# Moving a mixture's router scores from normalised rows at its start to raw rows at the end of the stage before it

## The reference

```python
def _layernorm(x, axis=-1, eps=1e-05):
    m = jnp.mean(x, axis=axis, keepdims=True)
    v = jnp.var(x, axis=axis, keepdims=True)
    return (x - m) / jnp.sqrt(v + eps)
...
x = x + 0.5 * _L0_ffn_ref(_layernorm(x), ...)     # three linear maps, tanh
x = x + _L0_attn_ref(_layernorm(x), ...)          # gated linear attention
x = x + 0.5 * _L0_ffn_ref(_layernorm(x), ...)
x = x + 0.5 * _L1_ffn_ref(_layernorm(x), ...)     # mixture, 1 of 8 experts
x = x + _L1_attn_ref(_layernorm(x), ...)
x = x + 0.5 * _L1_ffn_ref(_layernorm(x), ...)
x = x + 0.5 * _L2_ffn_ref(_layernorm(x), ...)     # mixture, 2 of 8 experts
x = x + _L2_attn_ref(_layernorm(x), ...)
x = x + 0.5 * _L2_ffn_ref(_layernorm(x), ...)
... # L3: dense experts, attention, dense experts
def _L1_ffn_ref(x, router_w, router_b, w1, b1, w2, b2, game_emb):
    logits = jnp.einsum('bsh,he->bse', x, router_w) + router_b
    expert_idx = jnp.argmax(logits, axis=-1)
    ... # each token's row through its expert: gelu((x + 0.1*game) @ w1 + b1) @ w2 + b2
def _L2_ffn_ref(x, router_w, w1, w2):
    probs = jax.nn.softmax(xf @ router_w.T, axis=-1)
    topv, topi = jax.lax.top_k(probs, 2)
    ... # the two experts' outputs, weighted
```

## Time and profile before

| | us |
|---|---|
| three runs, median | 1935.78 |
| three runs, lowest and highest | 1935.43 and 1937.0 |
| the profiled execution | 1927.49 |
| its span, first to last instruction | 1925.7 |
| around the span | 1.8 |

### The profile page before, as it was taken

How to read it: one execution, slowest core, us unless ns; L and a number is a source line. 1 busy time by engine, 2 the same in 40 slices (tenths; PEclk the granted TensorE clock), 3 DMA queues, 4 the chain that set the end, 5 groups by cost and what they waited for, 6 DMA issues and landing times. The chain is left out here.

```text
span 1925.7 us, 27869 instructions
## 1 busy us (share of the span) xinstructions
PE 1505.0 (78%) x9104; PEld 825.5 (43%) x9104; DVE 1106.2 (57%) x2420; ACT 918.3 (48%) x2114; POOL 358.5 (19%) x514
## 2 busy tenths in 40 slices
PE   4795748999999493882899999973883948999667
PEld 3344643555555482881222222223773532222345
DVE  6576432333433526215988888957214758878466
ACT  3553334444444151223688888761222327777422
POOL 0230630000000170771311010000671001100000
PEclk7796878999999595896899999995896978999878
DMA  2003444020200454546122020003452042220000
GB/s 70 5 1 94 140 127 99 1 66 5 61 1 1 136 145 124 155 135 172 41 42 68 10 77 1 1 1 97 135 150 72 1 129 77 78 77 1 1 0 22
DMA packets 96335, 126.08 MB, mean 65 GB/s; under 512 B 14773, under 2 KB 65973, under 8 KB 95693
## 3 DMA queue, kind: packets, MB, share of 16 engines
q1 hardware_dynamic: 86540, 105.26, 19.3%
q0 software_dynamic: 7936, 16.27, 3.1%
q10 hardware_dynamic: 1728, 2.88, 0.7%
HBM read 87.57 MB, written 36.80 MB: 65 GB/s over the span
## 5 line engine op out<-in xcount | busy, mean ns | idle before, releaser
L1944 DVE TENSOR_REDUCE MAXI<-psum 128x2 f32<-128x1024 f32 x384 | 457.2, 1219 | 91.0 <-PE psum L1752 88.1
L1861 ACT ACTIVATE EX<-psum 128x512 f32<-128x512 f32 x768 | 412.8, 605 | 104.6 <-PE psum L1773 104.5
L1773 PE MATMUL psum<-QM,KM 64*128 64x512 bf16 x768 | 227.2, 384 | 28.9 <-ACT EX L1861 21.7
L2209 PE MATMUL psum<-EX,N 128*128 128x512 f32 x512 | 237.6, 607 | 0.0
L2267 ACT ACTIVATE EX<-psum 128x512 f32<-128x512 f32 x256 | 149.4, 599 | 173.2 <-PE psum L2201 173.2
L1752 PE MATMUL psum<-KM,QS 64*128 64x512 bf16 x768 | 184.7, 401 | 37.1 <-DVE MAXI L1944 15.5
L1783 PE MATMUL psum<-EX,VST 128*32 128x512 f32 x1536 | 203.1, 604 | 1.0 <-ACT OT L1875 1.0
L1048 POOL DMA_INDIRECT m_XG<-rows,m_ROWS x124 | 121.8, 983 | 389.3 <-DVE m_ROWS L1263 352.7
L1080 PE MATMUL psum<-m_XT,m_W 128*128 128x128 f32 x992 | 144.0, 291 | 23.7 <-DVE m_XT L1294 19.0
L1301 DVE TENSOR_SCALAR m_Y<-psum 128x128 f32<-128x128 f32 x124 | 36.1, 291 | 215.7 <-DMA y<-m_Y,m_ROWS 136.0
L285 PE MATMUL psum<-ident,N 128*128 128x128 f32 x192 | 46.1, 406 | 138.1 <-DVE N L249 137.8
(11 more groups left out here) (303 smaller groups left out, 2127.6 us busy)
## 6 DMA issues: line engine op xcount, KB each, us to landing
m_W<-in_w_dram SPq DMA_DIRECT2D x124, 256.0 KB, 2.9
parts<-PART SPq DMA_DIRECT2D x36, 256.0 KB, 2.3
m_DOWN<-in_w_dram SPq DMA_DIRECT2D x32, 256.0 KB, 4.7
parts<-PART SPq DMA_DIRECT2D x12, 384.0 KB, 2.5
parts<-PART SPq DMA_DIRECT2D x36, 128.0 KB, 2.1
rows<-N SPq DMA_DIRECT2D x16, 256.0 KB, 4.7
N<-y SPq DMA_DIRECT2D x16, 256.0 KB, 4.1
parts<-FIX SPq DMA_DIRECT2D x16, 256.0 KB, 3.0
```

What stands on the lines that cost most here:

```text
L1773: pe.matmul(bank_of(("score", n, i)), KM[r, buf, g, m, kt * P:(kt + 1) * P], QM[r, n % 2, MAPS[at] // slots, :], start=True, stop=True).th ...
L1861: act.activation(EX[:, n % 2, kt, MAPS[j], :], bank_of(("score", n, i)), ACT.Exp, scale=SM_SCALE).then_inc(S["exp"].sem, 1)
L1944: dve.tensor_reduce(MAXI[:, n % 2, qt, columns], pair(i), AX, ALU.max, negate=True).then_inc(S["reduced"].sem, 1)
L2209: last = pe.matmul(banks[4 + j], N[:, n // per_b * TB + kt, :], EX[:, n % 2, kt, j, :], start=kt == 0, stop=kt == TB - 1)
```

## The change

It has five parts.

1. `load` also loads both routers and makes `CENTRE` = identity - 1/128. TensorE multiplies it with the 16 router columns, ScalarE copies the result to `centred`.
2. The stage in front of a mixture ends with `score_ahead` on TensorE and `take_ahead` on ScalarE: T of a block of **X** as soon as its BN_STATS are done (into banks 0 and 1 in turn), the copy to `nT`, and S with the centred columns into bank 2. The order is that of before, T0 T1 S0 T2 S1 T3 S2 S3.
3. A mixture starts with `norm_scale` on VectorE (reciprocal, shift), then one operation that multiplies all scores by 1/s, then the wait for the small loads and the routing chain. ScalarE alone writes the 16 tiles of N.
4. The constants `ONESB`, `RESET` and `UPTOB` are made on GpSimd. `COLS` is made behind the first half of the routing chain.
5. The second mixture, which is followed by the third, puts 28 products whose results nobody reads (`unread`) on TensorE between its last expert and `score_ahead`: 12 at once, 10 after the scatters, 6 after the first block of results is back.

A few semaphores are also merged or renamed (`heads` into `headrows`, `cumstep` into `step`, one `stage_load`).

```diff
@@ load @@
+                for k in range(2):
+                    sp.dma_start(self.routers[:, k, :], a[f"router{k + 1}"]).then_inc(consts.sem, 16)
+
+            @block.tensor
+            def _(pe):
+                pe.wait_ge(consts.sem, 64)
+                pe.wait_ge(centre.sem, 1)
+                pe.matmul(self.banks[7][:, 0:2 * E], self.CENTRE[:], self.routers[:].rearrange("p k e -> p (k e)"),
+                          start=True, stop=True).then_inc(centre.sem, 1)
+                pe.wait_ge(centre.sem, 3)
+                self.score_ahead(pe)
...
+                act.activation(self.centred[:].rearrange("p k e -> p (k e)"), self.banks[7][:, 0:2 * E], ACT.Copy
+                               ).then_inc(centre.sem, 1)
...
+                dve.tensor_scalar(self.CENTRE[:], self.ident[:], -1.0 / C, None, ALU.add).then_inc(centre.sem, 1)
@@ new functions @@
+    def score_ahead(self, pe):
...
+        def scores(b):
+            pe.wait_ge(S["columns"].sem, S["columns"].at(b + 1))
+            for t in range(b * TB, (b + 1) * TB):
+                last = pe.matmul(banks[2][:, t * E:(t + 1) * E], self.nT[:, t * P:(t + 1) * P],
+                                 self.centred[:, self.routes - 1, :], start=True, stop=True)
+            last.then_inc(S["scored"].sem, 1)
+
+        for b in range(B):
+            pe.wait_ge(self.norm["stats"].sem, self.norm["stats"].at(b + 1))
+            if b >= 2:
+                pe.wait_ge(S["columns"].sem, S["columns"].at(b - 1))
+            for j in range(TB):
+                last = pe.transpose(banks[b % 2][:, j * P:(j + 1) * P], self.X[:, b * TB + j, :], self.ident[:])
+            last.then_inc(S["turned"].sem, 1)
+            if b:
+                scores(b - 1)
+        scores(B - 1)
...
+        act.wait_ge(S["turned"].sem, S["turned"].at(b + 1))
+        act.activation(self.nT[:, b * L:(b + 1) * L], self.banks[b % 2], ACT.Copy).then_inc(S["columns"].sem, 1)
...
+    def norm_all_rows(self, act):
...
+        self.norm_root(act)
+        act.wait_ge(S["shift"].sem, S["shift"].at(1))
+        for b in range(B):
+            for t in range(b * TB, (b + 1) * TB):
+                last = act.activation(self.N[:, t, :], self.X[:, t, :], ACT.Identity, bias=rs[:, 3, t:t + 1],
+                                      scale=rs[:, 2, t:t + 1])
+            last.then_inc(S["rows"].sem, 1)
@@ end of attention1, TensorE @@
+                pe.wait_ge(S["exp"].sem, at8("exp", items - 1, 7))
+                self.score_ahead(pe)
@@ moe @@
-        aux = [(router[:], f"router{kind}"), (fixed[:], f"fixed{kind}"), (UPTO[:], "upto")]
+        aux = [(fixed[:], f"fixed{kind}"), (UPTO[:], "upto")]
...
-                for b in range(B):
-                    self.norm_turn(pe, b)
-                    if b == 1:
-                        pe.wait_ge(small.sem, small.at(16 * len(aux)))
-                    if b:
-                        scores(b - 1)
-                scores(B - 1)
-
+                def unread(bank, n):
+                    for _ in range(n):
+                        pe.matmul(banks[bank], self.identb[:], OHS[:, 0:4, :].rearrange("p m t -> p (m t)"),
+                                  start=True, stop=True)
+
+                pe.wait_ge(S["constants"].sem, S["constants"].at(2))
                 pe.wait_ge(S["chosen"].sem, S["chosen"].at(1))
...
+                if self.routes:
+                    unread(3, 12)
+                    for i in range(3):
+                        pe.wait_ge(scattered[i].sem, scattered[i].at(16 * len(range(i, R, 3))))
+                    unread(3, 10)
+                    pe.wait_ge(back[0].sem, back[0].at(16 * K))
+                    unread(3, 6)
+                self.score_ahead(pe)
...
-                self.norm_columns(act)
+                self.norm_all_rows(act)
...
-                self.norm_rows(dve)
-                dve.memset(ONESB[:], 1.0)
-                ch.link(dve.memset(RESET[:], 1.0))
-                dve.memset(RESET[:, :, 0:1], 0.0)
+                self.norm_scale(dve)
+                scored = self.ahead["scored"]
+                dve.wait_ge(scored.sem, scored.at(B))
+                ch.link(dve.tensor_tensor(logits, banks[2][:, 0:NT * E].rearrange("p (t e) -> p t e", e=E),
+                                          over(self.rs[:, 2, :]), ALU.mult))
                 dve.wait_ge(small.sem, small.at(16 * len(aux)))
-                dve.tensor_scalar(UPTOB[:], UPTO[:], 1.0, None, ALU.subtract)
-                dve.tensor_copy(COLS[:], const["cols"])
-                dve.wait_ge(S["scored"].sem, S["scored"].at(B))
```

More of the change, by code:

```diff
@@ L150, in __init__ @@
         self.gla_follows = self.last = False
+        self.routes = None
+        self.routers = sb("routers", [P, 2, E])
+        self.centred = sb("centred", [P, 2, E])
+        self.CENTRE = sb("CENTRE", [P, P])
+        self.ahead = {n: self.semaphore_of(f"ahead_{n}") for n in "turned columns".split()}
+        self.ahead["scored"] = self.semaphore_of("route_scored")
         names = "fresh stats moments variance root shift rows rows_act turned ready".split()
@@ L239, in moments_passed @@
         self.norm["moments"].passed(B)
+    def score_ahead(self, pe):
+        if not self.routes:
+            return
+        S, banks = self.ahead, self.banks
+        def scores(b):
[14 more added lines that the diff above has]
+        scores(B - 1)
@@ new lines, in take_ahead, with ahead_passed, norm_scale @@
+    def take_ahead(self, act, b):
+        if not self.routes:
+            return
+        S = self.ahead
+        act.wait_ge(S["turned"].sem, S["turned"].at(b + 1))
+        act.activation(self.nT[:, b * L:(b + 1) * L], self.banks[b % 2], ACT.Copy).then_inc(S["columns"].sem, 1)
+    def ahead_passed(self):
+        if self.routes:
+            self.ahead["turned"].passed(B)
+            self.ahead["columns"].passed(B)
+    def norm_scale(self, dve):
+        S, rs = self.norm, self.rs
+        dve.wait_ge(S["root"].sem, S["root"].at(1))
+        dve.reciprocal(rs[:, 2, :], rs[:, 1, :]).then_inc(S["variance"].sem, 1)
+        dve.wait_ge(S["variance"].sem, S["variance"].at(1))
+        dve.scalar_tensor_tensor(out=rs[:, 3, :], in0=self.mv[:, :, 0], scalar=-1.0, in1=rs[:, 2, :],
+                                 op0=ALU.mult, op1=ALU.mult).then_inc(S["shift"].sem, 1)
@@ new lines, in norm_all_rows, with norm_rows_passed @@
+    def norm_all_rows(self, act):
+        S, rs = self.norm, self.rs
+        self.norm_root(act)
+        act.wait_ge(S["shift"].sem, S["shift"].at(1))
+        for b in range(B):
+            for t in range(b * TB, (b + 1) * TB):
+                last = act.activation(self.N[:, t, :], self.X[:, t, :], ACT.Identity, bias=rs[:, 3, t:t + 1],
+                                      scale=rs[:, 2, t:t + 1])
+            last.then_inc(S["rows"].sem, 1)
+    def norm_rows_passed(self):
+        S = self.norm
+        for n in ("variance", "root", "shift"):
+            S[n].passed(1)
+        S["rows"].passed(B)
@@ L1044, in _ @@
             def _(pool):
+                pool.memset(ONESB[:], 1.0)
+                pool.memset(RESET[:, :, 1:M], 1.0)
+                pool.memset(RESET[:, :, 0:1], 0.0).then_inc(S["constants"].sem, 1)
+                pool.wait_ge(small.sem, small.at(16 * len(aux)))
+                pool.tensor_scalar(UPTOB[:], UPTO[:], 1.0, None, ALU.subtract).then_inc(S["constants"].sem, 1)
                 def gather(r):
@@ L1103, in bias @@
                               ).then_inc(S["bias"].sem, 1)
-                def scores(b):
-                    self.norm_ready(pe, b)
-                    for t in range(b * TB, (b + 1) * TB):
-                        last = pe.matmul(banks[0][:, t * E:(t + 1) * E], nT[:, t * P:(t + 1) * P], router[:],
-                                         start=True, stop=True)
-                    last.then_inc(S["scored"].sem, 1)
-                for b in range(B):
-                    self.norm_turn(pe, b)
-                    if b == 1:
-                        pe.wait_ge(small.sem, small.at(16 * len(aux)))
-                    if b:
-                        scores(b - 1)
-                scores(B - 1)
+                def unread(bank, n):
[3 more added lines that the diff above has]
+                pe.wait_ge(S["constants"].sem, S["constants"].at(2))
                 pe.wait_ge(S["chosen"].sem, S["chosen"].at(1))
@@ L1181, in _ @@
                         last.then_inc(S["mixed"].sem, 1)
+                        if b:
+                            self.take_ahead(act, b - 1)
+                    self.take_ahead(act, B - 1)
+                else:
+                    for b in range(B):
+                        self.take_ahead(act, b)
             @block.vector
@@ L1339, in _ @@
                 counts["step"] = ch.n
-        S["scored"].passed(B)
+        self.ahead["scored"].passed(B)
+        S["constants"].passed(2)
         for n in ("chosen", "ranked", "placed", "inverted", "indexed", "experts"):
```

51 lines of the change are left out of this document (34 added, 17 removed).

## The result

The changed kernel takes 1914.24 us in the median of four runs (1911.3 to 1918.12), the kernel before, beside it, 1935.61 (1931.77 to 1937.0). The medians lie 21.4 us apart; the ratio of the runs is 0.9897, 95% interval 0.988 to 0.9914, which is 19.9 us less. A later set gave 1916.0 against 1935.37, ratio 0.9895 (0.9876 to 0.9913). The forecast was 1920.3 with a range of 1912 to 1927. The profiled execution of the changed kernel took 1911.3 us (span 1909.4), that of the kernel before 1927.49. The two profiles differ by 16.2 us and the medians by 21.4, because executions of either kernel scatter over 7 to 10 us.

The account below looks back on a forecast made before the run. Entries were taken as bound by the routing chain's wait for scores from TensorE at its lower clock. 35.9 gained at entries, less 19.5 in tails and 0.9 in the load stage, is 15.5 us: 1935.78 to 1920.3, range 1912 to 1927.

Parts of the forecast that it names:

- The bound at the entries: At each mixture's entry the routing chain waits for score products, TensorE late; after the change, for the small loads.
- The entries' gain: From square root to first routing operation at the four mixture entries: 58.2 us falls to 22.3, gaining 35.9 us.
- Kind 2: Two of the four mixtures, third and fourth: entry to routing chain put at 3.15 us instead of 12.10.
- kind 1: Two of the four mixtures, first and second: entry to routing chain put at 8.0 us instead of 17.00.
- The tails' loss: Ends of stages 2, 4, 5, 7: score work ahead of the barrier delays entries by 6.1, 4.6, 5.1, 3.7, together 19.5 us.
- the rival with the upper clock: Upper clock holds through the tails of stages 4, 5, 7: 13.4 us lost, 21.6 less in all, 1914.2 us; chance 0.22.
- the rival of the weights: Mixture loops become bound by later down loads, starting 8.5 us later four times: slower, 1970.7 us; chance 0.03.
- The load stage: A product and a copy behind VectorE's last work in the load stage cost 0.9 us, between 0.3 and 1.5.
- What was costed at nothing: ScalarE's 16 tiles, stores of N, down and up loads, GpSimd constants, COLS and unread products: hidden, no time cost.
- The serial tail: Transposes, copies and scores run one after another in the tails, moving entries 37.9 us together: 1938.7 us; chance 0.04.

Follow-up runs that it names:

- the kernel with three wide products: The changed kernel plus three unread 512-column products in stage 2, ahead of the first raw transpose: 1986.1 us, ratio 0.9895 to the kernel before.
- the first set: Runs of scores behind the barrier, no unread products, three products in stage 2, and small arrays kept, where the kernel before took 2006.9 us.

## Why the prediction was right

- **The bound at the entries.** Right. With the scores ready, the first routing operation waits for the small loads in all four mixtures; keeping these arrays moved it to +1 us.
- **The entries' gain, 35.9 us.** It is 36.7 us (58.05 less 21.33). Kind 2 was put at 3.15 us and is 2.55, kind 1 at 8.0 and is 7.9 and 8.3. The load of UPTO, issued as second rather than third, was seen 1.05 us earlier, where one issue less was put at 0.42.
- **The tails' loss, 19.5 us.** The term that was mis-sized: 15.6 us in one profile and 17.0 in the other, between the forecast and the 13.4 of the rival with the upper clock. Stage 2 was put at 6.1 and cost 5.9, stage 5 at 5.1 and cost 4.6 and 5.2. The step that failed is that in stage 4 and 7 the clock would fall half way through the five groups: in stage 4 it held to the end in both profiles (2.7 us, not 4.6), in stage 7 it held to the end in one and fell in the last group in the other (2.4 and 3.2, not 3.7). I had read from the kernel before that the clock falls 2.4 us after TensorE goes idle. With the transposes and scores in that place it fell 6.4 us after the attention's last product (632.65 to 639.1). I took "does not raise the clock" for "does not hold it"; the runs show a third thing, with this work the clock stays for some microseconds longer and may still fall in it. Nor is the delay fixed. In the kernel before, stage 2's clock fell 4.1 us after TensorE's last load there ended (163.3 to 167.4):

```profile
167.00:168.00 1.00, 0.00 (x0) 0.00 (x0) 1.00 (x9) 0.10 (x1) 0.00 (x0) 0.70 0.00 0
```

- **Two readings of rows.** The fall in stage 4 of the kernel before is no case against the idle pause: TensorE had stopped at 629.37 and did nothing in the slice in which it fell (0.00 busy). The case against it is the fall at full work in the kernel with three wide products. And the 274 GB/s of the rival of the weights stand in the earlier trace rows, not the earlier trace rows; the sum is right.
- **The rival in which the clock holds** gave 1914.2, the measured median, but that is luck in part: stage 5 lost the clock as forecast. The entries gave 0.8 us more than forecast, the tails took 2.5 to 3.9 less, the load stage 0.4 more; the rest lies within the scatter of the executions.
- **The load stage, 0.9 us.** 1.3 in the first profile (entry at 10.35 instead of 9.05), 0.7 to 1.3 in the others, of which the changed kernel's own are the two highest.
- **What was costed at nothing.** Right: the down loads were put at 8.8 us after the entry and start at 7.4, the first gather at 25.1 (kind 2) and starts at 24.6, and it waits for the row list; up and down products wait for no DMA of weights. ScalarE's tiles take 0.39 us each, not 0.487, since 16 in a row take 6.3 us.
- **The serial tail and the weights** did not come about; L278's products overlap the next transposes, and the gather had its time to spare.

## What to carry to other kernels

When the last wait of a handoff is taken away, look up what releases the same instruction a little earlier: here the small loads stood 1.6 to 7.4 us behind the scores, and keeping them resident was worth another 14 us by the ratios. Ask, too, what each wait covers: almost half of this change's gain was score products that waited for arrays which they don't read. Transposes and score products took almost twice as long behind a pause as right behind dense work (3.54 against 1.92 us for the same sixteen loads), so put such work at the end of a dense stage. Products that nobody reads helped in two tails with pauses, showed no gain in a third, and cost 1.4 us in the one without a pause. Move work to another stage by its distances at both ends: in this case the sum of a few distances gave the gain of eleven kernels, one of them measured twice, to within 4 us.

## What the runs showed of the hardware

- Transposes and 8-column products kept TensorE busy for 10.24 of 10.30 us at a granted clock of 0.50 and never raised it, at each of the four entries; the same kind of work ran at 1.00 through all of stage 4's tail, to 5.7 us behind the attention's last product (632.65 to 638.36).
- The granted clock fell from 1.00 to 0.50 while TensorE was busy (1.00 of 1.00 us in 175 to 176, 3.00 of 3.00 behind it), 4.8 us behind the last 512-column product. With two or three 512-column products between the groups it was still 1.00 after 7 to 11 us, and then fell in stage 2 with TensorE busy again, 1.3 us behind the last of them.
- One and the same kernel, the kernel before, took 2006.9 us in the first set and 1935.4 and 1932.4 in the two later ones. It is not the chip by its number: the first and the third set are both on record for chip 11. In all four profiles of the first set the mixtures' expert loops hold stalls of VectorE and ScalarE whose releaser the profile calls remote; no profile of the other sets has such a line. In the kernel without unread products, by the waits view (total us, times, longest):

```profile
DVE m_Y L1398 <- remote: 117.3, 27, 5.6
ACT m_H L1262 <- remote: 86.3, 28, 5.8
```

What these stalls are, and what brought them on, no run here shows; the entries agree between the sets to within 0.4 us and the tail of stage 4 to 0.01.
